# In every step the unit of projections, V, Wo or FFN is issued ahead of P.V instead of behind it

## What is computed

```
q, k, v = x @ Wq[h], x @ Wk[h], x @ Wv[h]             # 16 heads, 64 wide
attn    = softmax(causal(q @ k.T / 8))                # 1024 x 1024 for each head and batch
heads   = attn @ v                                    # "P.V"
y       = LN(x + heads @ Wo, eps 1e-3) * gamma + beta
x1      = LN(x + y, eps 1e-5)
h       = silu(x1 @ Wg.T / 127) * (x1 @ Wu.T / 127)   # int8-valued weights
out     = LN(x1 + h @ Wd.T / 127)
```

## Time and profile before

| | |
|---|---|
| median of three runs | 1559.93 us |
| the profiled execution, as a timed run | 1562.23 us |
| its span on the chip | 1560.2 us |
| PE busy | 1479.8 us (95%) |
| GpSimd (POOL) busy | 1031.2 us (66%) |
| ScalarE (ACT) busy | 1012.5 us (65%) |
| VectorE (DVE) busy | 890.3 us (57%) |
| mean granted TensorE clock | 0.979 |

### The profile page before, as it was taken

The page is one execution under the profiler, slowest core; times in us unless marked ns, Lnnn a source line. Parts: engine busy times, 40 slices in busy tenths (PEclk is TensorE's granted clock), DMA queues, the critical chain, the costliest instruction groups (busy, mean ns, idle before and its releaser), DMA issues.

```text
span 1560.2 us, 24106 instructions
## 1 busy us (share of the span) xinstructions
PE 1479.8 (95%) x8576; PEld 1264.0 (81%) x8576; DVE 890.3 (57%) x1814; ACT 1012.5 (65%) x1921; POOL 1031.2 (66%) x980
## 2 busy tenths in 40 slices
PE   6899999999989999999999999999999999999746
PEld 5778888888878888888888888888888888888546
DVE  7645555555545665655566565556656555564246
ACT  3666777767666676766667676666767666676332
POOL 2666666666676675767667575776757576677664
PEclk9999999999999999999999999999999999999869
DMA  3322222321332221321232122132232212221000
GB/s 122 95 76 55 89 62 89 102 56 52 113 107 77 56 89 48 92 72 43 81 109 89 49 68 68 43 109 55 89 102 61 70 49 82 55 62 48 28 1 28
DMA packets 61143, 110.88 MB, mean 71 GB/s; under 512 B 16096, under 2 KB 41440, under 8 KB 61024
## 3 DMA queue, kind: packets, MB, share of 16 engines
q1 hardware_dynamic: 61024, 109.35, 23.6%
HBM read 61.34 MB, written 13.89 MB: 48 GB/s over the span
## 4 chain that ended last, share of the span: by engine, by line
PE 82%; POOL 7%; DVE 7%; issue 2%; ACT 1%; DMA 1%; SPq 0%; ACTq 0%; POOLq 0%; DVEq 0%
PE bank L660 22%; PE bank L633 15%; PE bank L527 11%; PE bank L603 8%; PE bank L588 7%; PE bank L552 6%; PE bank L706 5%; PE bank L718 3%; POOL probs_lo L1122 3%; PE bank L641 2%; PE bank L610 2%; DVE max_part L959 1%; POOL h_lo L1164 1%; DVE tanh_h L1019 1%; DVE tanh_h L1016 1%
## 5 line engine op out<-in xcount | busy, mean ns | idle before, releaser
L1122 POOL TENSOR_TENSOR probs_lo<-probs,probs_hi 128x512 fp32r<-128x512 f32 x576 | 738.9, 1289 | 443.4 <-ACT probs_hi L812 442.9
L959 DVE TENSOR_REDUCE max_part<-bank 128x1 f32<-128x512 f32 (+2 forms) x640 | 361.5, 582 | 362.9 <-PE bank L610 231.7
L809 ACT ACTIVATE probs<-bank 128x512 f32<-128x512 f32 x576 | 344.4, 598 | 294.8 <-PE bank L641 199.1
L633 PE MATMUL bank<-Q,K 128*128 128x512 f32 (+3 forms) x1536 | 385.7, 353 | 7.0 <-issue 4.0
L812 ACT ACTIVATE probs_hi<-bank 128x512 fp32r<-128x512 f32 x576 | 342.2, 594 | 0.0
L633 PEld LDWEIGHTS bank<-Q,K 128*128 128x128 f32 x1536 | 253.7, 190 | 36.0 <-issue 7.7
L660 PE MATMUL bank<-probs_hi,VH 128*128 128x512 f32 (+3 forms) x768 | 257.0, 375 | 6.5 <-POOL probs_lo L1122 6.2
L603 PE MATMUL bank<-K,Q 128*128 128x512 f32 (+3 forms) x768 | 247.4, 363 | 5.5 <-DVE neg_max L973 3.0
L660 PE MATMUL bank<-probs_hi,VL 128*128 128x512 f32 (+3 forms) x768 | 235.5, 347 | 0.0
L660 PE MATMUL bank<-probs_lo,VH 128*128 128x512 f32 (+3 forms) x768 | 235.2, 347 | 0.0
L603 PEld LDWEIGHTS bank<-K,Q 128*128 128x128 f32 x768 | 136.2, 190 | 33.0 <-DVE neg_max L973 3.4
(11 more groups left out here) (135 smaller groups left out, 2348.7 us busy)
## 6 DMA issues: line engine op xcount, KB each, us to landing
Q<-Q SPq DMA_DIRECT2D x64, 256.0 KB, 3.5
K<-K SPq DMA_DIRECT2D x64, 256.0 KB, 3.4
recip_bc<-recip_scratch SPq DMA_DIRECT2D x64, 256.0 KB, 3.4
wh<-w_scratch SPq DMA_DIRECT2D x12, 768.0 KB, 4.4
wl<-w_scratch SPq DMA_DIRECT2D x12, 768.0 KB, 6.0
wo_quad<-wo SPq DMA_DIRECT2D x16, 256.0 KB, 3.0
y<-x SPq DMA_DIRECT2D x4, 1024.0 KB, 5.5
x_tail<-x SPq DMA_DIRECT2D x13, 256.0 KB, 3.0
```

What stands on the lines that cost most here:

```text
L633: last = mm(bk[:, at:at + cols], KX[:, n, P * i:P * i + P], QX[:, n, q0:q0 + cols], start=(KX is K1 and at == 0), stop=(KX is K2 and k not ...
L809: A(pe_[:, g % 2, :], stb[g % 2][:, :], ACT.Exp).then_inc(exp_done, 1)
L959: last = V.reduce_max(mp[:, j, c:c + 1], bk[:, at:at + cols], AX.X)
L1122: G.tensor_tensor(pl[:, g % RING, :], pe_[:, g % 2, :], ph[:, g % RING, :].bitcast(F32), ALU.subtract).then_inc(lo_done, 1)
```

## The change

`pv(g - LAG)` moves within TensorE's step from ahead of the units to behind them. Nothing else is changed: the same instructions with the same waits, and the order on the four other engines and of the DMAs is the same row for row.

```
                 if 0 <= h < NH and k in MDIAG:
                     max_mask(h, k)
-                if 0 <= g - LAG < NG:
-                    pv(g - LAG)
                 for n, gset, ts, at in tails(g):
                     ...
                     if v_due(g, u) is not None:
                         v_unit(v_due(g, u), u)
+                if 0 <= g - LAG < NG:
+                    pv(g - LAG)
```

## The result

The changed kernel takes 1581.96 us (median of four runs, 1579.05 to 1584.07) against 1561.0 us for the kernel before, measured beside it: a ratio of 1.0127, 95% interval 1.0099 to 1.0155. It is slower by 1.3%. The forecast was 1582.1 us. The profiled execution took 1582.63 us as a timed run, its span is 1580.6 us, 20.4 us longer than that of before (1560.2 us).

What follows compares the result with a forecast made beforehand. TensorE's instructions were taken to bound the kernel's middle. The terms 14.0 + 7.7 + 1.6 + 2.6 - 3.7 = 22.2 us on the median of 1559.93 gave 1582.1 us; own range 1575 to 1589, eight in ten 1574 to 1593.

Steps and rivals of the forecast that it cites:

- What bounds, and the mechanism: TensorE's instructions bound the middle; units hanging on scores or maxima between lose 0.70 us, those hanging on earlier units don't.
- Down products, 20 x 0.70: Steps 26 and 32 of iterations 5 to 14: TensorE waits 0.70 us more in each, 14.0 us in all.
- Wo's first quarter: Step 11, waiting for L1019 held behind the maxima: eleven times 0.70 us, 7.7 us lost.
- 0.8 to 1.0 had been named as the sign: In the waits list, PE's L718 would wait for L1164 some 25 times at 0.8 to 1.0 us.
- step 12 costs nothing: Down products of step 12: cost put at nothing, as step 11's wait has pushed TensorE behind their inputs.
- Up products, 1.6 us: Step 9: first weight load uncovered, 0.1 to 0.2 us, 11 times, 1.6 us; bounds 0 to 2.8.
- Ahead of iteration 5, -3.7 us: Gain in step 11: 1.2 us in iterations 1 to 3, about 0.1 in iteration 4; bounds -2.5 and -4.6.
- Iteration 15: Down products of steps 21, 25, 31 and 35: 0.65 us lost each, 2.6 us; bounds 1.5 to 3.0.
- the rival of the falling clock: New waits lower the granted clock once per iteration in eleven iterations: 17 us more, about 1599 us; chance 0.08.
- 22.5: Loss in us over iterations 5 to 14: down products 14.0, Wo's first quarter 7.0, up products 1.5.
- The waits did not move along: Rival: every unit's inputs come 0.70 us earlier too, leaving only the gain, 1556.2 us; chance 0.05.
- More late units: Rival: two to four further places in 16 iterations wait 0.15 to 0.3 us, about 1591 us; chance 0.12.

Runs made afterwards that it cites:

- The split: Two products of P.V ahead of the units and the third behind them in every step, against the kernel before: 1569.75 us, ratio 1.0041.
- the single step: P.V behind the unit only in step 26 of iterations 5 to 14, against the kernel before: 1568.52 against 1561.88 us, ratio 1.0043.
- the GLU ahead of the maxima: The changed kernel with VectorE's three GLU operations ahead of the row maxima of their step: 1560.53 us, ratio 0.9989 to the kernel before.
- the kernel with only the late units: Kernel before with P.V behind the unit only in step 11 from iteration 5 on and in down-product steps: 1585.53 against 1562.44 us.
- the complement: Kernel before with P.V behind the unit everywhere except step 11 from iteration 5 on and down-product steps: 1559.74 against 1562.44 us, ratio 0.9979.

## Why the prediction was right, and where it was off

**What bounds, and the mechanism.** Right. The units whose inputs hang on the maxima between lost 0.7 us each, the others moved with their inputs. The split, the single step and the GLU ahead of the maxima each show it from another side, the last by taking the cause away.

**Down products, 20 x 0.70, and Wo's first quarter.** Right. PE waits in iteration 11 are 0.69 us in step 26 (1083.47), 0.83 in step 32 and 0.86 in step 11; for the first two 0.8 to 1.0 had been named as the sign. One step alone cost 6.6 us in ten iterations where 7.0 were put down. That step 12 costs nothing held as well: PE's waits of L718 between the cuts are 20, those of steps 26 and 32.

**Up products, 1.6 us.** Too large. Three times 0.70 make all of the +2.10 us of an iteration, and the kernel with only the late units comes to +2.02; the complement loses its 0.09 at this step. So step 9 costs about 0.1 us, 0.8 to 0.9 us in ten. L1012 of step 8 ends at 1037.08 in the changed kernel, and the first up product is there at 1037.18; what nothing covers is a tenth of a microsecond, the lower bound of the term.

**Ahead of iteration 5, -3.7 us.** Too small; measured is -5.0. Iterations 1, 2 and 3 are shorter by 1.29, 1.35 and 1.27 us instead of 1.2, and iteration 4 up to its step 26 by 0.51, not by 0.1: together -4.4, inside the bound of -4.6. Two terms were mis-sized. The 0.25 us for a weight load of Wo that nothing covers was too much: in iteration 1 TensorE arrives at 145.56 in the changed kernel and Wo starts at 145.66. And iteration 4 won twice the 0.25 us that its P.V had waited; what the other half is these runs don't show.

The remaining 0.6 us are not the change's. Some 0.24 us lie ahead of iteration 1, whose first scores come between 118.77 and 119.93 in four kernels with one and the same order up to there, and 0.36 behind step 26 of iteration 4, where TensorE waits 3.96 us for issue before and 3.94 after. The stretch around this wait (columns as in the earlier trace rows), before:

```profile
430.00:450.00 20.00, 16.04 (x78) 13.10 (x77) 6.02 (x13) 9.62 (x19) 13.16 (x13) 0.83 0.58 177
```

and after:

```profile
430.00:450.00 20.00, 16.34 (x88) 13.56 (x89) 6.82 (x14) 9.73 (x19) 13.71 (x12) 0.91 0.38 116
```

At the lower level of half the full clock, shares of 0.83 and 0.91 over 20 us are 6.8 and 3.6 us. The kernel with only the late units settles that the order of TensorE isn't the cause: its order there is that of the kernel before, and it takes 26.88 us from the scores of step 26 to iteration 5 where the kernel before takes 27.50, at the clock of the changed one:

```profile
430.00:450.00 20.00, 15.59 (x86) 12.71 (x85) 5.98 (x12) 9.64 (x18) 13.85 (x13) 0.91 0.57 166
```

The first scores of iteration 5 lie between 457.91 and 459.25 in the four kernels that keep P.V ahead in the early steps, so a microsecond moves on its own.

**Iteration 15.** Nearly right for the waits: they make 4.4 - 1.5 = 2.9 us where 3.4 were forecast. The kernel with only the late units, whose clock doesn't fall, is 3.3 us behind when it comes to the down products of step 39 (96.27 us from the second cut for 92.97), as forecast. The changed kernel gets some of it back there, which the forecast had not seen: its wait of L718 in step 39 is 2.57 us instead of 3.26, as in every kernel here with the whole P.V behind the up products of step 36. The 1.5 us of clock came on top; they are the rival of the falling clock, in one place instead of eleven.

**The total.** There are three misses: 22.5 for 21.0 and -3.7 for -5.0, which make the forecast 1.5 and 1.3 us too high, and 3.4 for 4.4, which makes it 1.0 too low: 1.8 us by the spans. The forecast for the median was 1582.1, the median is 1581.96; that they meet to 0.1 us is luck, since the three misses partly cancel and the median of the kernel before, measured again beside the changed one, is 1.1 us higher too.

**The rivals.** The waits did not move along: L1016 in step 24 comes after the maxima. They do in step 30 once VectorE's order is changed, and in part in step 24, where L973 still stands ahead. More late units did not show: PE's waits for L931 stand at 4.0 us in three places, as before, and none for L935 has come in. Only in iteration 3 is there one new wait, 0.40 us of Wo's first quarter for L1128, inside the gain of that iteration. The clock fell once behind a new wait, not eleven times. Through the middle it was 1.00 with waits of 0.7 to 0.9 us three times in each iteration. What the Trainium skill says of clocks that go back and forth on short idles between groups of matmuls (TensorE: Matmul & The Clock Gate, "A second HAM failure mode: psum-queue depth-cycling") this trace doesn't bear out for such waits.

## What to carry to other kernels

Before a unit is moved ahead on an engine, ask of each of its inputs on what it hangs: on the unit before it in the same chain, which moves too, or on something between that stays; only the second costs, and then the whole of what was taken out of the distance. Look for the cause in the order of the engine that makes the input: an instruction that is ready and stands behind one that waits (here the GLU behind the row maxima) can be worth more moved than the consumer: with it moved the kernel before became 7.5 us faster, and the changed kernel came back to the time of the kernel before. Where an order is good in a few steps and bad in others, take it in those few, and look at the seams, since a mixture changes distances that neither pure order has.

## What the runs showed of the hardware

**The same waits, another clock.** In iteration 15 the changed kernel, the one with the GLU first and the one with only the late units all have P.V behind the down products, and PE waits 1.33, 1.71 and 1.21 us, 1.33, 1.71 and 1.21, and 1.34, 1.58 and 1.20. In the first the clock was 0.58 for 4 us behind the second of these, in the two others 1.00 (a row of the one is shown above). In the third:

```profile
1469.00:1480.00 11.00, 9.80 (x68) 8.81 (x69) 2.96 (x5) 5.92 (x11) 8.95 (x8) 1.00 0.08 26
```

So the length of the waits alone doesn't decide whether the clock falls. What does isn't settled by these runs. A difference of 1 to 3 us between kernels of this length should not be put down to their code before the granted clock of the places has been looked at; the changed kernel's own timed runs lie 5 us apart.

**A load that seems hidden.** In the kernel before, three weight loads in each iteration started 0.4 to 0.6 us late while P.V was running, and only one of them left the matmuls idle for as much as 0.15 us. Yet they cost 0.2 to 0.33 us of TensorE's time each: 0.74 us in an iteration came back when the three inputs were on time.
